# Maxima in pairs: one VectorE read of two PSUM banks in place of two reads of one

## The reference

```python
scores = jnp.einsum('bqhd,bkhd->bhqk', q, k) * scale      # cross: 512 x 1601 for each head
attn = jax.nn.softmax(scores, axis=-1)                    # needs the maximum of each query's row
out = jnp.einsum('bhqk,bkhd->bqhd', attn, v)
...
causal = jnp.triu(jnp.ones((S, S), bool), k=1)            # self: 512 x 512, upper part masked
scores = jnp.where(causal, -jnp.inf, scores)
attn = jax.nn.softmax(scores, axis=-1)
```

## Time and profile before

| what | value |
|---|---|
| three runs | median 3208.35 us (3205.2 to 3213.45) |
| the profiled execution's own time | 3208.35 us |
| its span | 3206.7 us |
| TensorE matmuls busy | 2653.5 us, 83% |
| TensorE weight loads busy | 1345.6 us, 42% |
| VectorE busy | 1813.1 us, 57% |
| ScalarE busy | 1433.4 us, 45% |
| cross attention, from its first piece to its last product | about 304 to 1586 us |
| self attention, first turn to last turn (31 units) | 1851.9 to 2191.2 us, about 11 us a unit |

### The profile page before, as it was taken

One profiled execution on the slowest core, in us unless ns is written; L12 is line 12 of the kernel. 1 busy time (PEld: TensorE's weight loads), 2 busy tenths in 40 slices (PEclk: granted clock), 3 DMA queues, 4 the chain that ended last, 5 costly groups with the idle time before them and its releaser, 6 DMA issues. The chain is left out here.

```text
span 3206.7 us, 58377 instructions
## 1 busy us (share of the span) xinstructions
PE 2653.5 (83%) x14654; PEld 1345.6 (42%) x14655; DVE 1813.1 (57%) x3856; ACT 1433.4 (45%) x2927; POOL 490.1 (15%) x650
## 2 busy tenths in 40 slices
PE   7996999999999999999769689885440599999980
PEld 5663233333333333333145344442330377777750
DVE  4564887878787878788256466663231122222223
ACT  2331576767676767677623256663110122212210
POOL 2445000000000000000034511110225200000006
PEclk9997899999999999999989899997665799999995
DMA  6777554545544544553046366663435111011116
GB/s 209 216 232 146 70 74 67 68 68 66 70 64 69 69 64 69 64 69 50 22 153 203 128 140 138 144 136 104 146 122 185 61 33 33 31 31 33 33 47 186
DMA packets 524824, 313.65 MB, mean 98 GB/s; under 512 B 312112, under 2 KB 486848, under 8 KB 524480
## 3 DMA queue, kind: packets, MB, share of 16 engines
q1 hardware_dynamic: 492752, 256.93, 39.4%
q0 software_dynamic: 11392, 37.76, 3.6%
q10 hardware_dynamic: 20464, 16.40, 1.6%
HBM read 188.91 MB, written 121.26 MB: 97 GB/s over the span
## 5 line engine op out<-in xcount | busy, mean ns | idle before, releaser
L717 DVE TENSOR_REDUCE att_cross_neg_max<-att_cross_ps_s 128x1 f32<-128x401 f32 x2048 | 1031.4, 567 | 217.6 <-PE att_cross_ps_s L636 215.0
L792 ACT ACTIVATE att_cross_probs<-att_cross_ps_st 128x512 f32<-128x512 f32 (+1 forms) x1664 | 883.0, 601 | 349.0 <-PE att_cross_ps_st L655 331.0
L636 PE MATMUL att_cross_ps_s<-att_cross_k_pack,att_cross_q_pack 96*128 96x401 bf16 x2048 | 666.8, 349 | 28.8 <-DMA att_cross_q_pack<-q_parts 28.3
L655 PE MATMUL att_cross_ps_st<-att_cross_q_pack,att_cross_k_pack 99*128 99x512 bf16 (+1 forms) x1664 | 642.6, 389 | 37.0 <-issue 30.8
L670 PE MATMUL att_cross_ps_o<-att_cross_probs,att_cross_v_tiles 128*32 128x512 f32 (+1 forms) x3328 | 452.4, 616 | 1.0
L636 PEld LDWEIGHTS att_cross_ps_s<-att_cross_k_pack,att_cross_q_pack 96*128 96x128 bf16 x2048 | 203.4, 99 | 402.7 <-DVE att_cross_neg_max L717 233.4
L655 PEld LDWEIGHTS att_cross_ps_st<-att_cross_q_pack,att_cross_k_pack 99*128 99x128 bf16 (+1 forms) x1664 | 165.7, 100 | 343.7 <-ACT att_cross_probs L792 194.8
L717 DVE TENSOR_REDUCE att_self_neg_max<-att_self_ps_s 128x1 f32<-128x128 f32 (+3 forms) x512 | 223.5, 485 | 140.8 <-PE att_self_ps_s L639 137.3
L792 ACT ACTIVATE att_self_probs<-att_self_ps_st 128x256 f32<-128x256 f32 (+3 forms) x512 | 205.7, 441 | 127.7 <-PE att_self_ps_st L658 118.8
L1742 DVE COPY moe_hiddenT<-moe_ps_h 128x256 f32<-128x256 f32 x142 | 60.2, 424 | 296.9 <-PE moe_ps_h L1652 296.9
L1706 ACT ACTIVATE moe_silu<-moe_ps_g 128x352 f32<-128x352 f32 x142 | 65.8, 463 | 301.0 <-PE moe_ps_u L1644 301.0
(11 more groups left out here) (208 smaller groups left out, 2906.0 us busy)
## 6 DMA issues: line engine op xcount, KB each, us to landing
att_cross_k_pack<-k_parts SPq DMA_DIRECT2D x192, 200.1 KB, 6.6
k_parts<-in_part SPq DMA_DIRECT2D x72, 256.0 KB, 3.2
in_rows<-in_ctx_dram SPq DMA_DIRECT2D x24, 512.0 KB, 4.2
v_rows<-in_v_biased SPq DMA_DIRECT2D x24, 512.0 KB, 2.9
att_cross_q_pack<-q_parts SPq DMA_DIRECT2D x192, 64.0 KB, 7.5
att_cross_v_tiles<-v_rows SPq DMA_DIRECT2D x128, 96.0 KB
att_self_k_pack<-k_parts SPq DMA_DIRECT2D x192, 64.0 KB, 3.1
att_self_q_pack<-q_parts SPq DMA_DIRECT2D x192, 64.0 KB, 3.2
```

Of the source, the lines that this page charges most:

```text
L636: mm = nc.tensor.matmul(ps_s[bank][:, 0:w], qp[v.buf][0:SROWS, j, q * P:(q + 1) * P], kp[v.buf][0:SROWS, j, s:s + w], start=True, stop=not ...
L655: mm = nc.tensor.matmul(ps_st[bank_of_step[s]][0:rows, q0:SEQ], kp[u.buf][0:MROWS, j, t * P:t * P + rows], qp[u.buf][0:MROWS, j, q0:SEQ], ...
L717: nc.vector.tensor_reduce(nmax[v.odd][:, j * QT + q, i:i + 1], ps_s[bank][:, 0:w], AX.X, ALU.max, negate=True).then_inc(s_read, 1)
L792: nc.scalar.activation(pr[0:rows, (u.odd * STEPS + s) % RING, q0:SEQ], ps_st[bank_of_step[s]][0:rows, q0:SEQ], ACT.Exp).then_inc(exp_done, 1)
```

## The change

In cross attention the four pieces of a query row become two pairs. `ps_s` is now two buffers of two banks each. TensorE fills both banks of a buffer with two matmuls of 401 columns, only the second of which signals, and VectorE reduces both banks with one instruction over two axes (`AX.XY`, 2 x 401 elements). A unit has 32 pairs in place of 64 pieces, and `nmax` holds two columns for each row; the merge is a `tensor_tensor` minimum of the two. In self attention a piece is still one bank wide, and uses the first bank of its buffer. In both, the slots rotate over 2 in place of 4; the turn takes one of these slots; the wait on `m_read` moves from piece KT + 3 to piece KT + 1; KT becomes 3 in cross attention, which leaves the turn at step 41.875.

```diff
-        pieces = [(j, q, 0, 0, (q + 1) * P) for j in range(GH) for q in range(QT)]
+        pieces = [(j, q, [(0, (q + 1) * P)]) for j in range(GH) for q in range(QT)]
...
-        PIECES = 4
-        span = -(-kv // PIECES)
-        starts = [min(i * (kv // PIECES), kv - span) for i in range(PIECES)]
-        pieces = [(j, q, i, starts[i], span) for j in range(GH) for q in range(QT) for i in range(PIECES)]
-    SBUFS = 4
+        span = -(-kv // 4)
+        starts = [min(i * (kv // 4), kv - span) for i in range(4)]
+        pieces = [(j, q, [(s, span) for s in starts[h * 2:h * 2 + 2]])
+                  for j in range(GH) for q in range(QT) for h in range(2)]
+        PIECES = 2
...
-    KT = 3 if causal else 6
+    KT = 3
...
-        ps_s = [p.ps(f"ps_s{i}", [P, SEQ]) for i in range(SBUFS)]
+        ps_s = [p.ps(f"ps_s{i}", [P, 2, SEQ]) for i in range(2)]
...
-            return (v.r * SLOTS + k + (k >= KT) - 1) % SBUFS
+            return (v.r * SLOTS + k + (k >= KT) - 1) % 2
...
-                        if what == "piece" and k == KT + SBUFS - 1:
+                        if what == "piece" and k == KT + 1:
                             pe.wait_ge(m_read, v.n)
                         else:
-                            turned_between = what == "piece" and KT <= k < KT + SBUFS - 1
-                            pe.wait_ge(s_read, v.n * NP + (k + 1 + turned_between))
-                        mm = nc.tensor.matmul(ps_s[bank][:, 0:w], qp[v.buf][0:SROWS, j, q * P:(q + 1) * P],
-                                              kp[v.buf][0:SROWS, j, s:s + w], start=True, stop=not causal)
+                            pe.wait_ge(s_read, v.n * NP + (k + 1 + (what == "piece" and k == KT)))
+                        for n, (s, w) in enumerate(spans):
+                            last = nc.tensor.matmul(ps_s[bank][:, n, 0:w], qp[v.buf][0:SROWS, j, q * P:(q + 1) * P],
+                                                    kp[v.buf][0:SROWS, j, s:s + w], start=True, stop=not causal)
...
-                        mm.then_inc(s_done, 1)
+                        last.then_inc(s_done, 1)
...
-                dve.sem_inc(s_read, SBUFS)
+                dve.sem_inc(s_read, 2)
...
-                        nc.vector.tensor_reduce(nm[:, :], nmax[v.odd][:, :, :], AX.X, ALU.min).then_inc(m_merged, 1)
+                        nc.vector.tensor_tensor(nm[:, :], nmax[v.odd][:, :, 0], nmax[v.odd][:, :, 1], ALU.min)\
+                          .then_inc(m_merged, 1)
...
-                    nc.vector.tensor_reduce(nmax[v.odd][:, j * QT + q, i:i + 1], ps_s[bank][:, 0:w], AX.X, ALU.max,
-                                            negate=True).then_inc(s_read, 1)
+                    nc.vector.tensor_reduce(nmax[v.odd][:, col, half:half + 1], ps_s[bank][:, 0:len(spans), 0:spans[0][1]],
+                                            AX.XY, ALU.max, negate=True).then_inc(s_read, 1)
```

More of the change, by code:

```diff
@@ L539, in bank_of @@
         def bank_of(v, k):
-            return (v.r * SLOTS + k + (k >= KT) - 1) % SBUFS
+            return (v.r * SLOTS + k + (k >= KT) - 1) % 2
         def bank_of_max(v, last):
-            return ((v.r + 1) * SLOTS - 1 + (0 if last else KT)) % SBUFS
+            return ((v.r + 1) * SLOTS - 1 + (0 if last else KT)) % 2
         def in_order(u, after):
@@ L625, in maxima @@
                     if what in ("piece", "piece0"):
-                        j, q, _, s, w = pieces[k]
-                        bank = bank_of(v, k) if what == "piece" else k % SBUFS
+                        j, q, spans = pieces[k]
+                        bank = bank_of(v, k) if what == "piece" else k % 2
                         if k == 0:
                             pe.wait_ge(kq_in[v.buf], v.loads(BUFS) * KQ)
-                        if what == "piece" and k == KT + SBUFS - 1:
+                        if what == "piece" and k == KT + 1:
                             pe.wait_ge(m_read, v.n)
                         else:
-                            turned_between = what == "piece" and KT <= k < KT + SBUFS - 1
-                            pe.wait_ge(s_read, v.n * NP + (k + 1 + turned_between))
-                        mm = nc.tensor.matmul(ps_s[bank][:, 0:w], qp[v.buf][0:SROWS, j, q * P:(q + 1) * P],
-                                              kp[v.buf][0:SROWS, j, s:s + w], start=True, stop=not causal)
-                        if causal:
-                            mm = nc.tensor.matmul(ps_s[bank][:, w - P:w], keep["ident_b"][:, :],
-                                                  keep["mask_q_b"][:, :], start=False, stop=True)
-                        mm.then_inc(s_done, 1)
+                            pe.wait_ge(s_read, v.n * NP + (k + 1 + (what == "piece" and k == KT)))
+                        for n, (s, w) in enumerate(spans):
+                            last = nc.tensor.matmul(ps_s[bank][:, n, 0:w], qp[v.buf][0:SROWS, j, q * P:(q + 1) * P],
+                                                    kp[v.buf][0:SROWS, j, s:s + w], start=True, stop=not causal)
+                            if causal:
+                                last = nc.tensor.matmul(ps_s[bank][:, n, w - P:w], keep["ident_b"][:, :],
+                                                        keep["mask_q_b"][:, :], start=False, stop=True)
+                        last.then_inc(s_done, 1)
                     elif what == "turn":
@@ L644, in maxima @@
                         pe.wait_ge(m_split, v.n + 1)
-                        nc.tensor.transpose(ps_s[bank_of_max(v, k)][:, 0:P // 2].bitcast(BF16),
+                        nc.tensor.transpose(ps_s[bank_of_max(v, k)][:, 0, 0:P // 2].bitcast(BF16),
                                             nm_parts[:, :, :].rearrange("p a q -> p (a q)"), keep["ident_b"][:, :])\
@@ L707, in maxima @@
                 def maxima(what, v, k):
-                    if what == "split" and PIECES > 1:
-                        dve.wait_ge(s_read, (v.n + 1) * NP + SBUFS)
-                        nc.vector.tensor_reduce(nm[:, :], nmax[v.odd][:, :, :], AX.X, ALU.min).then_inc(m_merged, 1)
+                    if what == "split" and PIECES == 2:
+                        dve.wait_ge(s_read, (v.n + 1) * NP + 2)
+                        nc.vector.tensor_tensor(nm[:, :], nmax[v.odd][:, :, 0], nmax[v.odd][:, :, 1], ALU.min)\
+                          .then_inc(m_merged, 1)
                     if what not in ("piece", "piece0"):
                         return
-                    j, q, i, _, w = pieces[k]
-                    at, bank = (turn(v, k), bank_of(v, k)) if what == "piece" else (k, k % SBUFS)
+                    j, q, spans = pieces[k]
+                    at, bank = (turn(v, k), bank_of(v, k)) if what == "piece" else (k, k % 2)
+                    col, half = j * QT + q, k % PIECES
                     dve.wait_ge(s_done, at + 1)
-                    nc.vector.tensor_reduce(nmax[v.odd][:, j * QT + q, i:i + 1], ps_s[bank][:, 0:w], AX.X, ALU.max,
-                                            negate=True).then_inc(s_read, 1)
+                    nc.vector.tensor_reduce(nmax[v.odd][:, col, half:half + 1], ps_s[bank][:, 0:len(spans), 0:spans[0][1]],
+                                            AX.XY, ALU.max, negate=True).then_inc(s_read, 1)
                 def unit(u, after):
@@ L754, in link @@
                         pool.wait_ge(m_step, v.n * LINKS + done[0])
-                    if PIECES > 1:
+                    if PIECES == 2:
                         pool.wait_ge(m_merged, v.n + 1)
@@ L759, in split @@
                     else:
-                        pool.wait_ge(s_read, (v.n + 1) * NP + SBUFS)
+                        pool.wait_ge(s_read, (v.n + 1) * NP + 2)
                         full = nmax[v.odd][:, :, 0]
@@ L797, in copy_max @@
                     act.wait_ge(m_rows_in, v.n * 16 + 1)
-                    nc.scalar.copy(nm_rows[:, :], ps_s[bank_of_max(v, last)][0:3 * GH * QT, 0:P // 2]
+                    nc.scalar.copy(nm_rows[:, :], ps_s[bank_of_max(v, last)][0:3 * GH * QT, 0, 0:P // 2]
                                    .bitcast(BF16)).then_inc(m_read, 1)
```

## The result

The changed kernel takes 3300.15 us (median of 4 runs, 3298.1 to 3301.28); the kernel before 3206.77 us beside it. The ratio is 1.0293, 95% interval 1.0265 to 1.0323: slower by 2.9%. The prediction was 3300, range 3250 to 3345, slower 0.92.

A forecast was written before the change was run, and what follows sets the result against it. TensorE was taken to bound cross attention, the longest stage, and a chain through a DMA to set self attention's loop. The profiled 3208 us + 65 (cross attention) + 26 (self attention) = 3299, said as 3300 us, range 3250 to 3345.

The forecast's parts named there:

- (a) The long read: VectorE's 802-element read in cross attention takes 1.00 us; VectorE's work falls 1.8 us a unit, counted as nothing.
- (b) The turnaround: Cross attention: a two-bank buffer can be overwritten only 1.60 us after its pair's first matmul, once its whole read ends.
- Triples: Six runs of three pairs without a product block between, in cross attention: stalls 4 x 0.29 + 2 x 0.08 = 1.32 us a unit.
- (c) The turn: Cross attention: the turn takes one of two slots, so pair 3 reuses pair 2's buffer and stalls 1.00 us.
- Cross sum: Cross attention's stalls, 1.32 + 1.00, taken as 2.2 us a unit: 68 us, less 3 at loop edges, 65 us.
- Self attention: Two of four buffers taken away: 0.94 us a unit, 29 us, less 3 at the loop's edges: 26 us (17 to 50).
- a leak behind the turn: Self attention: of 1.07 us of stalls beside the DMA's wait, 0.3 us a unit leaks; 0 if it always covers.
- VectorE as the bound: Rival: TensorE waited for VectorE, so the change makes the kernel faster, -55 us, 3153; chance 0.05.
- Only the turn stalls: Rival: the triples just fit in cross attention, 31 x 1.0 + 26 = +57 us, 3265; chance 0.12.
- No change: Rival: ScalarE's slack and TensorE's own gaps take the stalls; time within 0.3%; chance 0.03.
- only cross attention: Rival: self attention leaks nothing or hides all, so only cross attention slows, 3273 to 3290; chance 0.12.
- The clock: Rival: stalls lower TensorE's clock, 3470 if once each unit, 3320 if only at edges; 3345 or more, chance 0.10.

The follow-up runs named there:

- e4: The kernel before, with VectorE reading only 200 of each 401 columns in all of cross attention: 3189.9 us, ratio 0.9966 to the kernel before.
- e6: The changed kernel with four pairs of cross attention moved by a quarter to half a step: 3279.5 us, ratio 1.0216 to the kernel before.
- e1: The changed kernel with the turn of cross attention one pair later (KT 4): 3272.9 us, ratio 1.0201 to the kernel before.
- e2: The changed kernel with four one-bank buffers again in self attention only: 3278.2 us, ratio 1.0215 to the kernel before.
- e8: The kernel before with two buffers instead of four in self attention only: 3222.7 us, ratio 1.0057 to the kernel before.
- e7: The changed kernel with one VectorE read for each bank, the buffer released after the second: 3305.6 us, ratio 1.0312 to the kernel before.
- e3: The changed kernel with VectorE reading 200 of each bank's 401 columns in cross attention: 3244.2 us, ratio 1.0111 to the kernel before.
- e9: The kernel before, reading 200 of 401 columns only in the first unit's 64 pieces of cross attention: 3193.3 us, ratio 0.9976 to the kernel before.

## Why the prediction was right

The forecast was a loss of 91 us; the medians lost 93.4, which is what the 68 of cross attention and the 25 of self attention make.

*The bound.* TensorE in the units, with e4 as the control: with VectorE's reads at 367 ns for 565 (medians) the units kept their length.

*(a) The long read.* Taken at 1.00 us, measured 0.988. Worth nothing, as said.

*(b) The turnaround.* Taken at 1.60 us, measured 1.60 at both places shown. Triples: the one shown stalled 0.26 for 0.29. e6 moved four of them and got 0.65 us a unit back, so their cost is shown, not only their presence. One sign that I had named for the stalls was wrong: idle time for VectorE of 60 to 70 us in this stage. It was 26, because the records of matmuls hide 0.17 us of each gap.

*(c) The turn.* Taken at 1.00 us, measured 0.97; e1 took away 1.00 us a unit by moving it behind a block. The wait for ScalarE's copy was covered, as said.

*Cross sum.* 2.2 us a unit, measured 2.26. I had taken 3 us off for the loop's edges; they gave nothing: the six units with an edge between their splits were 45.9 to 47.7 us long and became 49.0 to 49.5, on average 2.3 longer, as much as the others. So 65 should have been 68, which is what was measured. That half the clock hides the stalls was a wrong step, of small size.

*Self attention.* Forecast 26; the traces say 25 (20.5 by the first pair alone), e2 and e8 moved the end by 22 and 17. The stalls ahead of the turn, 0.64 x 31 = 20, are the larger part. The term of 0.3 us a unit for a leak behind the turn was mis-sized: the loop grew by 0.71 us a unit on average, which leaves 0.07 for it. The DMA's wait took most of it, and the bound "0 if it always covers" was the nearer end. How much leaks is open, for loops with the same buffers differ by 5 to 7 us from trace to trace. In its place stand 3.0 us that the sum did not have: the first unit's pieces, ahead of the first turn, took 11.7 us for 8.7.

*The total.* Cross attention was put 3 us too low, the first unit's 3 us were left out, and the loop of self attention was put some 4 too high. These errors nearly cancel. That the two stages slow down for these reasons was foreseen; that the total came out within 3 us was partly luck.

*Rivals.* VectorE as the bound is refuted by e4 and e7, except in the start of the stage. "Only the turn stalls" is refuted by e6. "No change" falls with the result, and "only cross attention" with e2 and e8. The clock: stalls of 1 us did not lower it (0.96 for 0.97 over 1200 us), so what the Trainium skill tells of a clock that swings with idle gaps from cycling through PSUM banks (TensorE: Matmul & The Clock Gate, "A second HAM failure mode: psum-queue depth-cycling") did not come about here.

The Trainium skill's sentence that breaking up instructions may let work be completed sooner, where an engine that is not saturated makes bubbles (Perfetto Trace Analysis, "Optimizing Scalar/DVE Operations"), was tried by e7, and the trace does not agree: two reads of 401 for one of 802 made a unit 39.61 us long for 39.24, since the buffer came free only after the second. What helps is an earlier release: with the pair's read shortened in e3 a unit was 1.48 us shorter, some 46 us of the loss, and with smaller reads that each free a bank of their own, as in the kernel before, 2.26.

## What to carry to other kernels

Before joining two reads of PSUM into one, ask which engine bounds the stage. If it is the writer, what counts is a buffer's turnaround (fill, read, hops) against the writer's time until it needs that buffer again, and two buffers of two banks are not four of one. Then look for the places where a slot is taken by something else: there depth two is depth one. If the depth must be small, put such places behind a long block of other work, as e1 did for 27 us, or more work between them, as e6 did for 21, both without touching an instruction. And breaking a read up helps only if a buffer comes free with each part (e7).

## What was not expected of the hardware

At the start of cross attention VectorE set the pace: TensorE began a 401-column matmul only every 0.45 us, though its records call it busy all the time, and the granted clock was at its lower level, 1.2 GHz. With the reads of that stretch made shorter in e9 it was mostly at the upper one, 2.4 GHz. The windows from 305 to 325 us, columns as in rows 2, of the kernel before and of e9:

```profile
305.00:325.00 20.00, 20.00 (x44) 4.46 (x42) 19.70 (x41) 0.00 (x0) 7.73 (x7) 0.50 1.09 128
```

```profile
305.00:325.00 20.00, 19.32 (x70) 7.08 (x68) 19.96 (x69) 0.00 (x0) 7.51 (x10) 0.89 1.09 119
```

44 matmuls began in the first and 70 in the second, where VectorE was again busy throughout (19.96 of 20 us), so the reads and not the clock set the pace there too. Shorter reads did not raise the clock by themselves: in e3, with two buffers of two banks, 52 matmuls began in this window and the clock stayed at 0.50. In the units of the changed kernel, with gaps of up to 1 us, it stayed up (0.96).
